# A selective-scan block behind a dynamic depthwise convolution: softplus' scratch moved into PSUM, its passes and silu's moved to other units

## The reference

```python
x = x + dynamic_depthwise_conv(group_norm(x))   # 7x7 filters made from the image itself: softmax key, two mixes, layer norm
x = x + vision_ssm(group_norm(x))
# vision_ssm
x, z = split(conv1x1(input))                    # 128 channels each
f1 = conv1x1(x); f2 = conv2x2_stride2(f1); f3 = conv2x2_stride2(f2)   # 1024, 256 and 64 positions
# at each level, forward and backward, with 16 states n:
delta = softplus(dts @ dtw + dtb)
h = h * exp(delta * A) + delta * B * x ;  y = sum_n h * C + x * D ;  y = layernorm(y)
y2 += upsample(y3);  y1 += upsample(y2)
out = conv1x1(y1 * silu(z))
```

## Time and profile before

| | |
|---|---|
| Median of 3 runs | 4017.46 us (4017.43 to 4022.0) |
| Profiled execution, its own time | 4034.78 us |
| Its span, first to last instruction | 4033.0 us |
| Busy shares: PE, DVE, ACT, POOL | 79%, 78%, 67%, 77% |
| Mean granted TensorE clock | 0.882 of full |
| DMA | 665 MB, 165 GB/s |

### The profile page before, as it was taken

The page is one execution under the profiler, slowest core; times in us unless marked ns, Lnnn a source line. Parts: engine busy times, 40 slices in busy tenths (PEclk is TensorE's granted clock), DMA queues, the critical chain, the costliest instruction groups (busy, mean ns, idle before and its releaser), DMA issues. The chain is left out here.

```text
span 4033.0 us, 54359 instructions
## 1 busy us (share of the span) xinstructions
PE 3185.3 (79%) x13644; PEld 1617.1 (40%) x13644; DVE 3157.4 (78%) x3847; ACT 2699.4 (67%) x6662; POOL 3106.8 (77%) x1588
## 2 busy tenths in 40 slices
PE   6978787987878798787978878798887879878522
PEld 3544344443434444344444434444443444443210
DVE  1068788787878878787887878788787878878787
ACT  4467776766777676777767776676777767676532
POOL 0059688796978969697896969789696887969787
PEclk8998898998889898898989889899888989988765
DMA  1035455553545545454553545455354545535454
GB/s 43 1 111 201 149 183 169 173 201 134 194 156 188 188 157 197 138 194 158 192 198 139 202 137 198 158 189 206 133 203 141 189 163 190 205 119 203 152 185 165
DMA packets 187326, 665.46 MB, mean 165 GB/s; under 512 B 22736, under 2 KB 24672, under 8 KB 186976
## 3 DMA queue, kind: packets, MB, share of 16 engines
q1 hardware_dynamic: 186976, 661.47, 47.4%
HBM read 639.76 MB, written 21.63 MB: 164 GB/s over the span
## 5 line engine op out<-in xcount | busy, mean ns | idle before, releaser
L832 PE MATMUL pconv<-pad,diag 128*128 128x464 f16 (+11 forms) x9408 | 2118.8, 380 | 154.6 <-ACT sg L1049 69.5
L832 PEld LDWEIGHTS pconv<-pad,diag 128*128 128x128 f16 x9408 | 932.8, 100 | 1291.4 <-issue 386.5
L1431 POOL TENSOR_TENSOR y<-y,h 128x1024 f32<-128x1024 f32 (+1 forms) x544 | 1231.3, 2263 | 184.3 <-DVE h L598 180.1
L1249 ACT ACTIVATE slot_b<-delta,nega 128x512 f32<-128x512 f32 (+1 forms) x1280 | 808.7, 640 | 837.3 <-DVE slot_c L589 602.1
L1396 POOL TENSOR_TENSOR bx<-bb,u 128x1024 f32<-128x1024 f32 x512 | 1223.6, 2391 | 0.9 <-DMA bb<-bc_rows 0.8
L589 DVE TENSOR_TENSOR_SCAN slot_c<-slot_b,bx 128x512 f32<-128x512 f32 (+1 forms) x768 | 784.8, 1044 | 219.5 <-POOL bx L1396 118.9
L598 DVE TENSOR_TENSOR h<-slot_c,cb 128x512 f32<-128x512 f32 x1152 | 773.6, 673 | 0.0
L589 DVE TENSOR_TENSOR_SCAN slot_c<-slot_b,slot_c,bx 128x512 f32<-128x512 f32 x512 | 663.7, 1296 | 78.4 <-ACT slot_b L1249 17.5
L1135 ACT ACTIVATE diag<-id,chi 128x128 f16<-128x128 f16 x1568 | 499.4, 387 | 2.3 <-PE pconv L832 1.8
L1135 ACT ACTIVATE diag<-id,clo 128x128 f16<-128x128 f16 x1568 | 497.8, 387 | 0.0
L1366 POOL TENSOR_TENSOR delta<-delta,rs 128x512 f32<-128x512 f32 (+1 forms) x96 | 97.9, 1019 | 313.1 <-DVE rs L536 313.1
(11 more groups left out here) (177 smaller groups left out, 3437.2 us busy)
## 6 DMA issues: line engine op xcount, KB each, us to landing
bb<-bc_rows SPq DMA_DIRECT2D x592, 512.0 KB, 4.5
cb<-bc_rows SPq DMA_DIRECT2D x592, 512.0 KB, 4.3
xr<-in_x SPq DMA_DIRECT2D x16, 1024.0 KB, 7.0
out<-ob SPq DMA_DIRECT2D x16, 1024.0 KB
bc_rows<-rows SPq DMA_DIRECT2D x64, 64.0 KB, 3.4
w<-in_w SPq DMA_DIRECT2D x2, 256.0 KB
wc<-in_wc SPq DMA_DIRECT2D x2, 256.0 KB
bc_rows<-rows SPq DMA_DIRECT2D x16, 32.0 KB, 4.0
```

What stands on the lines that cost most here:

```text
L832: ins = nc.tensor.matmul(img(bank(pconv, k), W)[:, r0:r1, c0:c1], w, pad[:, t, part, 16 * k + r0 + dy:16 * k + r1 + dy, c0 + dx:c1 + dx], ...
L1249: ins = nc.scalar.activation(slot_b[:, o:o + w], delta[:, so + c:so + c + w], ACT.Exp, scale=nega[:, st, n0 + n:n0 + n + 1])
L1431: pool.tensor_tensor(yv, yv, src[:, 0] if len(src.shape) == 3 else src, ALU.add).then_inc(q_y.sem, 1)
```

## The change

- `qs` shrinks to 256 columns a place. For chunks 2 to 5, q = 1 + e, its logarithm and the difference q - er are now kept in PSUM, in the bank of `pm` in which the chunk's v stood (`chunk_bank`: bank 0 for chunk 4, bank 1 otherwise). Chunks 0 and 1 are as before.
- `chunk` is parted into `chunk_bc` and `chunk_dt`, `chunk_exp` into `chunk_rows` and `chunk_exp`. In unit 0 only chunk 3's rows are made; its delta matmul waits for chunk 2's minimum and stands in unit 1 behind half of the taps, its ScalarE passes at the end of unit 1. `chunk_bc` of 4 and 5 stand at the end of unit 13 on TensorE, behind the unit's taps; their rows are copied at the start of unit 14 on ScalarE, ahead of the decays; both `chunk_dt` come in unit 14 behind its first tap, `chunk_exp(4)` at the end of unit 14 and `chunk_exp(5)` at the end of unit 15.
- On VectorE `chunk_first(c)` is the first instruction of units 1, 2, 15 and 16 for c = 2, 3, 4, 5, and `chunk_last(c)` stands ahead of the last half of the same unit. Before, they stood in the middle or at the end of units.
- Whatever else uses `pm` waits for `chunk_last` instead of for ScalarE's max(v, 0), and the key and filter steps of image m from unit 15 on, with the norms 2 and 3 of y, move by one unit.
- silu's ScalarE passes move from units 5 and 6 to 2 and 3, its GpSimd product from 7 to 4.

```diff
-        es, qs, rs = (sb(n, [P, 2, HALF]) for n in ("es", "qs", "rs"))
+        es, rs = (sb(n, [P, 2, HALF]) for n in ("es", "rs"))
+        qs = sb("qs", [P, 2, L2])
+        def chunk_bank(c):
+            return bank(pm, 0 if c == 4 else 1)[:, 0:CHUNKS[c][1]]
+        def chunk_q(c):
+            return qs[:, c, 0:CHUNKS[c][1]] if c < 2 else chunk_bank(c)
...
-                nc.vector.scalar_tensor_tensor(er[:, k, 0:n], qs[:, k, 0:n], 1.0, es[:, k, 0:n], ALU.subtract,
+                nc.vector.scalar_tensor_tensor(er[:, k, 0:n], chunk_q(c), 1.0, es[:, k, 0:n], ALU.subtract,
...
-                nc.vector.tensor_tensor(er[:, k, 0:n], qs[:, k, 0:n], er[:, k, 0:n], ALU.subtract).then_inc(ch_sub.sem, 1)
+                rest = er[:, k, 0:n] if c < 2 else chunk_q(c)
+                nc.vector.tensor_tensor(rest, chunk_q(c), er[:, k, 0:n], ALU.subtract).then_inc(ch_sub.sem, 1)
                 dve.wait_ge(ch_sub.sem, ch_sub.at(i, c + 1))
-                nc.vector.tensor_tensor(er[:, k, 0:n], er[:, k, 0:n], es[:, k, 0:n], ALU.min).then_inc(ch_min.sem, 1)
+                nc.vector.tensor_tensor(er[:, k, 0:n], rest, es[:, k, 0:n], ALU.min).then_inc(ch_min.sem, 1)
...
                 for q, p in halves_of(k):
-                    if k in CHUNK_MID and (q, p) == halves_of(k)[2]:
-                        chunk_first(i, CHUNK_MID[k])
+                    if k in CHUNK_AT and (q, p) == halves_of(k)[0]:
+                        chunk_first(i, CHUNK_AT[k])
+                    if k in CHUNK_AT and (q, p) == halves_of(k)[-1]:
+                        chunk_last(i, CHUNK_AT[k])
...
-            pre = {3: a_s0, 17: a_max_, 19: a_dg_, 20: a_ktc_, 21: a_fic_, 22: a_f2c_, 27: a_scale_}
+            pre = {3: a_s0, 18: a_max_, 20: a_dg_, 21: a_ktc_, 22: a_fic_, 23: a_f2c_, 28: a_scale_}
...
+            def chunk_bc(i, c):
+                if c == 0:
+                    pe.wait_ge(b_f.sem, b_f.at(i, 3))
+                else:
+                    pe.wait_ge(ch_rows.sem, ch_rows.at(i, min(c, 4)))
+                if c == 2:
+                    pe.wait_ge(b_z.sem, b_z.at(i, 1))
+                    pe.wait_ge(z_clip.sem, z_clip.at(i, 1))
+                if c in (4, 5):
+                    pe.wait_ge(n_o.sem, n_o.at(i, STEPS[2]))
+                nc.tensor.matmul(bank(pm, 1 if c == 5 else 0)[0:2 * NS, 0:n], wbc[:, st, :], f[:, fc:fc + n], start=True, stop=True).then_inc(ch_bc.sem, 1)
+            def chunk_dt(i, c):
+                if c == 1:
+                    pe.wait_ge(ch_pos.sem, ch_pos.at(i, 1))
+                if c == 3:
+                    pe.wait_ge(ch_min.sem, ch_min.at(i, 3))
+                if c in (4, 5):
+                    pe.wait_ge(ch_rows.sem, ch_rows.at(i, c + 1))
+                nc.tensor.matmul(chunk_bank(c), wdelta[:, st, :], f[:, fc:fc + n], start=True, stop=True).then_inc(ch_dt.sem, 1)
...
                 if i is not None:
-                    if k in CHUNK_PE:
-                        chunk(i, CHUNK_PE[k])
-                    if k == 1:
-                        flat_init(i)
+                    if k == 0:
+                        chunk_bc(i, 3)
+                    if k == 14:
+                        chunk_dt(i, 4)
+                        chunk_dt(i, 5)
...
                     taps(j, mid, some)
+                if i is not None and k == 1:
+                    chunk_dt(i, 3)
+                    flat_init(i)
...
-                    if i is not None and k in (5, 15):
-                        pe.wait_ge(ch_pos.sem, ch_pos.at(i, {5: 4, 15: NCH}[k]))
-                        pe.wait_ge(ch_rows.sem, ch_rows.at(i, {5: 4, 15: NCH}[k]))
+                    if i is not None and k in (5, 16):
+                        pe.wait_ge(ch_min.sem, ch_min.at(i, {5: 4, 16: NCH}[k]))
                     pre[k](m)
+                if i is not None and k == 13:
+                    chunk_bc(i, 4)
+                    chunk_bc(i, 5)
...
                 act.wait_ge(ch_exp.sem, ch_exp.at(i, c + 1))
-                nc.scalar.activation(qs[:, k, 0:n], es[:, k, 0:n], ACT.Identity, bias=1.0).then_inc(ch_q.sem, 1)
+                if c >= 2:
+                    act.wait_ge(ch_pos.sem, ch_pos.at(i, c + 1))
+                nc.scalar.activation(chunk_q(c), es[:, k, 0:n], ACT.Identity, bias=1.0).then_inc(ch_q.sem, 1)
...
-                    if k in CHUNK_LAST:
-                        chunk_log(i, CHUNK_LAST[k])
+                    if k in CHUNK_AT:
+                        chunk_log(i, CHUNK_AT[k])
+                    if k == 14:
+                        chunk_rows(i, 4)
+                        chunk_rows(i, 5)
                     if 1 <= k < NU - 1:
                         decay(i, k + 1, 0)
...
-                    if k in CHUNK_PE:
-                        chunk_exp(i, CHUNK_PE[k])
+                    if k == 0:
+                        chunk_rows(i, 3)
+                    if k in CHUNK_EXP:
+                        chunk_exp(i, CHUNK_EXP[k])
                     if k == 1:
                         keep_x(i)
...
-                    if k == 5:
+                    if k == 2:
                         silu_exp(i)
-                    if k == 6:
+                    if k == 3:
                         silu_end(i)
...
-                    if k == 7:
+                    if k == 4:
                         silu_end(i)
...
-CHUNK_PE = {0: 3, 13: 4, 14: 5}
-CHUNK_MID = {1: 2, 2: 3}
-CHUNK_FIRST = {14: 4, 15: 5}
-CHUNK_LAST = {1: 2, 2: 3, 15: 4, 16: 5}
+CHUNK_EXP = {1: 3, 14: 4, 15: 5}
+CHUNK_AT = {1: 2, 2: 3, 15: 4, 16: 5}
...
-NORM_ACT_RT = {9: 0, 12: 1, 29: 2, 32: 3}
-NORM_DVE = {10: 0, 13: 1, 30: 2, 33: 3}
+NORM_ACT_RT = {9: 0, 12: 1, 30: 2, 33: 3}
+NORM_DVE = {10: 0, 13: 1, 31: 2, 34: 3}
```

More of the change, by code:

```diff
@@ L698, in unit @@
                     products(i, k)
-                    if k in CHUNK_FIRST:
-                        chunk_first(i, CHUNK_FIRST[k])
-                    if k in CHUNK_LAST:
-                        chunk_last(i, CHUNK_LAST[k])
                     if k in NORM_DVE:
@@ L935, in bridge @@
                 if j is not None:
-                    chunk(j, 0)
+                    chunk_bc(j, 0)
+                    chunk_dt(j, 0)
                 if i is not None:
@@ L940, in bridge @@
                 if j is not None:
-                    chunk(j, 1)
+                    chunk_bc(j, 1)
+                    chunk_dt(j, 1)
                 if i is not None:
@@ L952, in bridge @@
                 if j is not None:
-                    chunk(j, 2)
+                    chunk_bc(j, 2)
+                    chunk_dt(j, 2)
             pre = {5: lambda m: sums1(m, sa, bank(pm, 1), a_sums, a_stats),
                    6: lambda m: sums2(m, sa, bank(pm, 1), a_sums, a_spread),
-                   15: a_key_, 16: lambda m: (a_turn(m, 0), a_turn(m, 1)), 17: lambda m: (a_turn(m, 2), a_turn(m, 3)),
-                   19: a_kt_, 20: a_fi_, 21: a_f2_, 22: a_sum3, 23: a_sum4, 25: a_wg_}
+                   16: a_key_, 17: lambda m: (a_turn(m, 0), a_turn(m, 1)), 18: lambda m: (a_turn(m, 2), a_turn(m, 3)),
+                   20: a_kt_, 21: a_fi_, 22: a_f2_, 23: a_sum3, 24: a_sum4, 26: a_wg_}
             def unit(i, j, m, k):
@@ L1192, in copy_z, with chunk_rows @@
                 nc.scalar.activation(sz[:, :], pm[:, :], ACT.Identity, bias=v_inz).then_inc(b_z.sem, 1)
-            def chunk_exp(i, c):
+            def chunk_rows(i, c):
                 s, n, fc, st = CHUNKS[c]
@@ L1199, in chunk_exp @@
                     act.wait_ge(ch_out[k].sem, ch_out[k].at(i, 16 * (c // 2)))
-                nc.scalar.activation(rows[:, k, 0:n], bank(pm, 0)[0:2 * NS, 0:n], ACT.Copy).then_inc(ch_rows.sem, 1)
+                nc.scalar.activation(rows[:, k, 0:n], bank(pm, 1 if c == 5 else 0)[0:2 * NS, 0:n], ACT.Copy).then_inc(ch_rows.sem, 1)
+            def chunk_exp(i, c):
+                s, n, fc, st = CHUNKS[c]
+                k = c % 2
                 act.wait_ge(ch_dt.sem, ch_dt.at(i, c + 1))
@@ L1203, in chunk_exp @@
                     act.wait_ge(ch_min.sem, ch_min.at(i, c - 1))
-                nc.scalar.activation(es[:, k, 0:n], bank(pm, 1)[:, 0:n], ACT.Abs, bias=v_dtb[:, st:st + 1]).then_inc(ch_abs.sem, 1)
-                nc.scalar.activation(delta[:, s:s + n], bank(pm, 1)[:, 0:n], ACT.Relu, bias=v_dtb[:, st:st + 1]).then_inc(ch_pos.sem, 1)
+                nc.scalar.activation(es[:, k, 0:n], chunk_bank(c), ACT.Abs, bias=v_dtb[:, st:st + 1]).then_inc(ch_abs.sem, 1)
+                nc.scalar.activation(delta[:, s:s + n], chunk_bank(c), ACT.Relu, bias=v_dtb[:, st:st + 1]).then_inc(ch_pos.sem, 1)
                 act.wait_ge(ch_abs.sem, ch_abs.at(i, c + 1))
@@ L1280, in bridge @@
                     copy_f(j, 2)
+                    chunk_rows(j, 0)
                     chunk_exp(j, 0)
@@ L1288, in bridge @@
                 if j is not None:
+                    chunk_rows(j, 1)
                     chunk_exp(j, 1)
@@ L1451, in unit @@
                                 gather(i, q)
-                    if k in CHUNK_LAST:
```

(9 more changed lines are left out.)

30 lines of the change are left out of this document (10 added, 20 removed).

## The result

The changed kernel takes 4050.64 us (median of 4, 4047.91 to 4061.14), the kernel before 4019.73 us (median of 4): ratio 1.008, 95% interval 1.0058 to 1.0101, 31 us slower. One execution of the kernel before, among those timed beside the experiments, took 7190 us in a slow state and counts in no ratio.

The account below looks back on a forecast made before the run. No engine is always busy; GpSimd sets the pace where fed, VectorE bounds level 2. 16 x 2.4 - 15 x 0.9 = +25 us on the profiled 4034.78 gives 4060, 0.4% less as median: 4042 us, range 3980 to 4085.

Parts of the forecast that it names:

- The passes: The changed VectorE softplus passes of chunks 2 to 5: 0.75, 0.69 and 0.67 us, no longer held by GpSimd's running instruction.
- Place A: Chunks 4 and 5, units 14 to 18: 1+e comes late, GpSimd loses 1.9 us an image, bounds -1.2 and +3.4.
- The waits: VectorE's idle time before `chunk_first` for 1+e: 5.6 us for chunk 4 in unit 15, 3.7 for chunk 5 in unit 16.
- Place B: Level 2, units 1 to 4, where VectorE is the bound: sum +0.5 us an image, bounds -0.6 and +2.
- The silu product: GpSimd's product moves from unit 7 into a wait in unit 4: -2.36 us an image.
- Chunk 3's wait: Level 2, unit 2: VectorE stands from 1223.0 to 1227.5 for chunk 3's 1+e, +4.5 us.
- Place C: The bridge to the next image with the units before it: -0.9 us an image, from -2.0 to +0.3.
- the two passes of the root: ScalarE's root of the third norm, 1.2 us, moves from its wait for `conv_add(1)` into the busy stretch.
- The sum: Whole kernel: 16 x 2.4 - 15 x 0.9 = +25 us, from Place A and Place B for 16 images, Place C for 15.
- My step from the profiled time to the median: Whole kernel: median taken 0.4% under the profiled execution, as before the change, so 4060 became 4042 us.
- the passes gain what they lose: Rival, whole kernel: with q ready when its unit begins, some 8 us an image faster, 3892 us; chance 0.12.
- TensorE is in time: Rival at tap 49 in Place A: q(4) before about 1062.5 turns +1.9 to -1.2, giving 3993 us; chance 0.18.

Follow-up runs that it names:

- tensor_early: Changed kernel with TensorE's four matmuls of chunks 4 and 5 behind unit 13's first tap, ahead of tap 49; 3999.66 us, ratio 0.9958.
- first_mid: Changed kernel with `chunk_first` in the middle of its unit and `chunk_last` at the unit's end; 3967.60 us, ratio 0.9877.
- q_in_sbuf: Changed kernel in its new order, but 1+e, its logarithm and the difference in SBUF again; 4126.19 us, ratio 1.0285.
- delta3_early: Changed kernel with chunk 3's delta matmul right behind unit 1's first tap on TensorE, two taps earlier; 4039.51 us, ratio 1.0051.
- the second profile: The kernel before, unchanged, profiled again; span 4025.0 us, 8 less than the first profile.
- both orders: Changed kernel with the edits of first_mid and tensor_early together; 3923.57 us, ratio 0.9762.
- norms_later: Kernel before with only norms 2 and 3 of y and image m's key and filter steps one unit later; 4006.68 us, ratio 0.9963.

## Why the prediction was right

- **The passes:** 0.689, 0.687 and 0.692 us measured for 0.75, 0.69 and 0.67. A surcharge for the PSUM source did not show: with GpSimd idle the same passes took 0.66 to 0.69 us from SBUF. That a pass in SBUF stands for GpSimd's running instruction, which the prediction only supposed, is shown by the rows above. On ScalarE I had the sign wrong. I took 0.05 us more per pass into PSUM, from an exponential whose scale is a column of a tile. Against the same instruction with SBUF on both sides it is faster: 602 and 579 ns above; by shape, the kernel before has

```profile
L1209 ACT ACTIVATE qs<-es 128x512 f32<-128x512 f32 x64 | 40.3, 630 | 2.0
...
L1215 ACT ACTIVATE qs<-qs 128x512 f32<-128x512 f32 x64 | 39.5, 617 | 16.3 <-DVE rs L526 16.3
```

  so the Trainium skill's note (ScalarE: Activation LUTs) that PSUM is the faster target was right here, by 28 ns; the logarithm gained 38 ns, with its source in PSUM as well. It is 4 us in all at most.
- **Place A:** +1.9 predicted, +1.87 in the image worked through, +2.42 on average, because the average of before holds short steps that the one image didn't show. The waits were 5.6 and 3.7 predicted, 5.87 and 3.60 measured. That TensorE's order is behind the first is shown by tensor_early (-3.4, predicted -3.1), and that the place of the waits costs the time by first_mid; the passes alone gain, by q_in_sbuf.
- **Place B:** +0.5 predicted, -0.42 measured. The silu product gave 2.16 (predicted 2.36 at most), shown alone. Chunk 3's wait was 5.3 instead of 4.5: I had left TensorE's late start of the loop's turn out, which delta3_early shows. The sum is still 0.9 better than mine because of the image that I followed. Its B took 68.7 us before, the shortest of the 14 images in the loop (68.7 to 73.0, mean 70.2); the same image took 71.0 after. That is +2.3, where my 0.5 and the 2.2 by which its wait of 6.7 exceeds 4.5 make 2.7. Against the mean of before, my +0.5 on 68.7 would have been -1.0; measured is -0.4, by the longer waits. So the terms held on that image, and it stood for the average badly.
- **Place C:** -0.9 predicted, -0.99 measured, -0.82 with that part alone. `conv_add(1)` came even earlier than I had it, 2.6 us by ScalarE's wait for it instead of 2.0. On GpSimd the step from `inputs(35)` to `inputs(36)` shrank by 1.7 us and the one over the bridge grew by 1.2, as long as the two passes of the root that I had moved there. C is not steady to a tenth: it is 114.5 in tensor_early, with the same steps in C.
- **The sum:** +25 us predicted, +31 measured between the medians, +14 between the two profiles. The spans are not good to 10 us here: the profiled execution of before lay at the long end (13 long steps of 16), and the other executions of that kernel in these runs lie between 4004 and 4033 us, apart from the one of 7190. Taking the second profile instead gives 22 us. My step from the profiled time to the median by a fixed share had no ground: it took the execution profiled after for 0.4% above its median, and it was 2 us under it (4048.86 and 4050.64, for 4060 and 4042 predicted). That 25 lies so near 31 is in part luck, since B was predicted 0.9 us an image too dear and A 0.5 too cheap, and something that the profiles don't show made up the rest. What makes the remaining 9 us stays open.
- **The rivals:** that the passes gain what they lose would need q in time; it wasn't in any of these kernels. The one with both orders comes nearest, with waits of 2.3, 0.9 and 1.3 us for chunks 3, 4 and 5 and 3924 us, where this rival gave 3892. That TensorE is in time, and (within 7 us) the time it would give, were borne out when it was brought about. The TensorE idle time of 12.18 us in front of the key matmuls (above, at 1076.79) and their 6.20 us, behind it, instead of 3.6 cost nothing visible in the changed kernel, whose C is that of norms_later; a late TensorE a few units on did cost 0.8 us in C in tensor_early.

## What to carry to other kernels

Making an instruction shorter on the engine that is behind can bring nothing if its new place in the queue puts it ahead of work that doesn't need its input: the wait is paid by everything behind it. Put such a pass as late in its unit as its consumer allows, and check each producer's place in its own queue, here two matmuls behind a tap that waits for another engine. Of a change with several parts, time the parts alone: silu's steps alone gained 0.7% (27 us), the norms 0.4% (15 us). If the parts add, the softplus part with its new order must then have cost 73 us to leave 31 us net, although PSUM as the place of 1+e is worth 76 us in that order. With two places in the order put right, the same change is 2.4% faster than the kernel before. And take a forecast for an average from the average: one image out of 14 was 1.5 us off it, as much as the whole forecast an image.

## What the runs showed of the hardware

- A VectorE pass with both inputs in SBUF that began while a GpSimd instruction ran ended 0.54 to 0.57 us after that instruction, in 288 of 305 cases; with GpSimd idle it took 0.66 to 0.69 us. Which of the two starts first is a race: GpSimd 0.13 us ahead made it 2.77 us, 0.54 us behind 1.15, and here that moves the pace of the whole loop by 2 us an image. With one input in PSUM the pass took 0.68 to 0.69 us in 192 of 192, half of them beside a running GpSimd instruction.
- TensorE started a turn of the hardware loop after 3.1 to 6.1 us of idle time in the profiles of before and after, different in each turn, with no releaser in the profile. It showed in chunk 3's wait (4.4 to 7.1 us) as long as the delta matmul stood behind the unit's first taps, and no more with the matmul two taps earlier (4.5).
- Behind 12.18 us of idle time, the eight matmuls of the key took 6.20 us; the granted clock was 0.50, the lower of its two levels, over the first 3.2 us of them and 0.58 over the whole, where they had taken 3.63 us at full clock in the kernel before.
